# Two squared-sum passes of an eight-core sequence kernel wait for each 128-token block instead of the whole tile

## What is computed

```
x1  = x + W_out( h * silu-like gate of h )        # h from a recurrence over the tokens
y   = layernorm(x1)                               # mean and variance over 1024 features
hh  = rmsnorm(y, gamma1)                          # feeds Wq and Wdown/Wup
u   = y + ( attention over 16 heads ) @ Wo + bo
h2  = rmsnorm(u, gamma2)                          # mean of u*u over 1024 features
g   = softmax(h2 @ Wg)                            # 8 experts
out = x1 + u + sum_e g[e] * ( h2 @ We[e] )
```

## Time and profile before

| what | value |
|---|---|
| three timed runs | 3840.75, 3917.0, 3954.0 us (median 3917.0) |
| the profiled execution, own time | 3841.9 us |
| its span, slowest core (core 1) | 3840.0 us; the eight cores 3800.6 to 3840.0 us |
| TensorE matmul busy | 2512.3 us, 65% of the span |
| VectorE busy | 1468.3 us, 38% |
| ScalarE busy | 869.4 us, 23% |
| mean granted TensorE clock | 0.769 of full speed on core 1 |
| DMA | 319.70 MB, 83 GB/s on average |

### The profile page before, as it was taken

The page is one execution under the profiler, slowest core; times in us unless marked ns, Lnnn a source line. Parts: engine busy times, 40 slices in busy tenths (PEclk is TensorE's granted clock), DMA queues, the critical chain, the costliest instruction groups (busy, mean ns, idle before and its releaser), DMA issues.

```text
span 3840.0 us, 35132 instructions; the slowest of 8 cores (3800.6 to 3840.0 us)
## 1 busy us (share of the span) xinstructions
PE 2512.3 (65%) x12352; PEld 1180.1 (31%) x12352; DVE 1468.3 (38%) x1817; ACT 869.4 (23%) x1642; POOL 79.9 (2%) x143
## 2 busy tenths in 40 slices
PE   3556766557775587745976559664696647965578
PEld 1223322233332333223332234322243223432234
DVE  1343223453234433344333443245432363234532
ACT  2232003321123201232023320233103421024210
POOL 0000000000000000000000000000000000000000
PEclk9766888757887688866888669885698857987579
DMA  8631671301421013310233003320032201412012
GB/s 170 147 85 44 137 181 54 110 3 68 149 84 70 23 66 132 110 44 23 88 120 122 23 23 114 115 101 23 22 145 96 101 10 44 153 67 88 1 66 110
DMA packets 44455, 319.70 MB, mean 83 GB/s; under 512 B 5048, under 2 KB 5304, under 8 KB 28928
## 3 DMA queue, kind: packets, MB, share of 16 engines
q0 software_dynamic: 35040, 283.53, 23.7%
q1 hardware_dynamic: 9248, 33.91, 2.3%
HBM read 301.07 MB, written 48.23 MB: 91 GB/s over the span
## 4 chain that ended last, share of the span: by engine, by line
PE 52%; DVE 20%; DMA 11%; ACT 7%; issue 6%; DVEq 3%; ACTq 1%; POOL 0%; POOLq 0%; SPq 0%
PE bank L1432 21%; DMA w<-wscr 3%; PE bank L1146 3%; DMA w<-we 3%; PE bank L835 3%; PE bank L616 3%; PE bank L1372 3%; PE bank L442 3%; PE bank L488 3%; DVE vpu L929 3%; DVE kpot L929 2%; DVE sstat L1030 2%; PE bank L964 2%; PE bank L967 2%; DVE xph L1040 2%
## 5 line engine op out<-in xcount | busy, mean ns | idle before, releaser
L1432 PE MATMUL bank<-qpg,w 128*128 128x512 bf16 x4096 | 912.7, 387 | 86.6 <-DMA w<-we 44.4
L1432 PEld LDWEIGHTS bank<-qpg,w 128*128 128x128 bf16 x4096 | 405.8, 99 | 602.1 <-issue 137.2
L1405 DVE TENSOR_TENSOR qpg<-xph,ybuf 128x4096 bf16<-128x4096 bf16 x64 | 282.4, 4423 | 506.3 <-PE bank L1432 506.3
L1449 ACT ACTIVATE acomb<-bank 128x512 f32<-128x512 f32 x64 | 38.3, 598 | 1140.8 <-PE bank L1432 1136.7
L1016 ACT ACTIVATE hfm<-bank,sstat 128x128 bf16<-128x128 f32 x512 | 139.3, 383 | 529.4 <-DVE sstat L990 529.4
L1063 PE MATMUL bank<-cpb_s,xph 128*128 128x128 bf16 x512 | 64.8, 306 | 246.6 <-DVE xph L1040 246.6
L524 PE MATMUL bank<-xph,w 128*128 128x512 bf16 x512 | 133.2, 407 | 124.1 <-DMA w<-wscr 69.1
L616 PE MATMUL bank<-ln1g,w 128*128 128x512 bf16 x512 | 125.3, 410 | 96.1 <-DMA w<-wscr 75.7
L914 PE MATMUL bank<-zb,wupb 64*128 64x512 bf16 x128 | 73.2, 585 | 156.6 <-DVE vpu L929 112.0
L929 DVE TENSOR_SCALAR kpot<-bank,cph_s 64x512 bf16<-64x512 f32 x128 | 95.1, 743 | 196.4 <-PE bank L914 192.5
L990 DVE TENSOR_REDUCE sstat<-bank 128x4 f32<-128x512 f32 x128 | 82.5, 686 | 199.8 <-PE bank L967 199.8
(11 more groups left out here) (139 smaller groups left out, 2925.4 us busy)
## 6 DMA issues: line engine op xcount, KB each, us to landing
w<-wscr POOLq DMA_DIRECT2D x105, 2048.0 KB, 8.1
wscr<-w POOLq DMA_DIRECT2D x15, 2048.0 KB, 9.5
w<-we POOLq DMA_DIRECT2D x8, 2048.0 KB, 21.5
out<-ybuf SPq DMA_DIRECT2D x16, 1024.0 KB, 4.0
slotA<-x SPq DMA_DIRECT2D x4, 2048.0 KB
slotB<-x SPq DMA_DIRECT2D x4, 2048.0 KB, 13.5
w<-w_inT POOLq DMA_DIRECT2D x1, 2048.0 KB, 27.1
w<-w_aT POOLq DMA_DIRECT2D x1, 2048.0 KB, 22.7
```

The costliest lines, as they stand in the source:

```text
L1405: r = v.tensor_tensor(qpg[:, (e % 2) * 4096:(e % 2) * 4096 + 4096] .rearrange("p (c q) -> p c q", q=512), h2v[:, :, :], ybuf[:, e * 512:(e ...
L1432: last_pe = pe.matmul(bk[:, :], wslice(wbuf, kc, mc), qpg[:, (e % 2) * 4096 + kc * 512: (e % 2) * 4096 + (kc + 1) * 512], start=(e == 0 an ...
```

## The change

In `f_l2v` the one reduction over 128x4096 becomes four reductions over 128x1024, one per block, each behind a wait for that block's second add, `("x1", t, b, 1)`. They stand at the same place of VectorE's order as the one did, behind all eight adds. In `f_l2s` and in `f_us` the wait for the last add of the tile is replaced by a wait ahead of each square for the second add of its own block. Nothing else is touched: the squares, their outputs, the short statistics operations and all DMAs are as before.

```diff
             def f_l2v(v, t=t, xv=xv):
-                v.wait_ge(s_ve.h, tok[("x1d", t)])
-                r = v.tensor_reduce(
-                    sstat[:, S_S1:S_S1 + 4],
-                    xv[:, :].rearrange("p (b f) -> p b f", f=1024),
-                    axis=AX, op=OP.add)
+                for b in range(NBLK):
+                    v.wait_ge(s_ve.h, tok[("x1", t, b, 1)])
+                    r = v.tensor_reduce(
+                        sstat[:, S_S1 + b:S_S1 + b + 1],
+                        xv[:, b * 1024:(b + 1) * 1024],
+                        axis=AX, op=OP.add)
                 s_ve.inc(r)
                 tok[("ln2sum", t)] = s_ve.n
             block.vector(f_l2v)

             def f_l2s(s, t=t, xv=xv):
-                s.wait_ge(s_ve.h, tok[("x1d", t)])
                 for b in range(NBLK):
+                    s.wait_ge(s_ve.h, tok[("x1", t, b, 1)])
                     last_s = s.activation(out=trash_[b], in_=xv[:, b * 1024:(b + 1) * 1024],
...
             def f_us(s, t=t):
-                s.wait_ge(s_ve.h, tok[("ud", t)])
                 dwait(s, "d_ot")
                 for b in range(NBLK):
+                    s.wait_ge(s_ve.h, tok[("u", t, b, 1)])
                     s.activation(out=trash_[b],
```

## The result

The changed kernel runs at a median of 3817.65 us (16 runs), the kernel before at 3843.4 us (17 runs). The ratio is 0.9944, with a 95% interval of 0.9923 to 0.9965: 0.56% less, or some 21.5 us of 3843.4, between 13 and 30 us. The profiled execution took 3807.42 us with a span of 3805.5 us on its slowest core (core 2); the eight cores lie between 3784.0 and 3805.5 us.

The account below looks back on a forecast made before the run. The prediction saw no saturated engine but a chain of stages whose stalls are saved in full. -24.9 + 0.4 = -24.5 us, taken from the median 3917.0, gave 3892.5 us, with a range of 3806 to 3932.

Parts of the forecast that it names:

- Part 1: ScalarE's squares of u (`f_us`): block-wise waits start the last square earlier, saving 3.11 us a tile, 24.9 us in 8.
- Part 2: ScalarE's squares of x1 (`f_l2s`): end about 3.1 us earlier, worth nothing beside the reduction, up to 3 us without it.
- Part 3: VectorE's four reductions (`f_l2v`) after the x1 adds: 4.60 us together, taken as +0.05 us a tile, 0.4 us in all.
- The sum: Whole kernel: -24.9 us from the squares of u and +0.4 us from the four reductions make -24.5 us.
- the clock rival: Gate matmuls after u: a shorter stall keeps TensorE's clock up, 1.3 us a tile, 10.5 us more, 3882; chance 0.06.
- the upper end of the gain: Whole kernel: top of the forecast's own range from the bounds, a gain of 16 to 27 us.
- the first tile given back: First tile's experts: waits for expert weights absorb that tile's gain alone, 3895; losing most of the whole gain, chance 0.05.
- Small reductions: Rival at LN2 on VectorE: four unoverlapped 1.21 us reductions cost about +0.5 us a tile, gain 21 us, 3896; chance 0.10.
- the adds are not disturbed: Denies the rival that squares stretch VectorE's adds at x1 and u: at twice the length +41 us, 3958; chance 0.03.
- nothing was given back: Denies the rival that TensorE waits later for weight loads at a fixed date: all lost is 3917; losing most, chance 0.05.
- Within 2%: Whole kernel: measured time differs from before by under about 78 us, what a measurement can tell from no change; chance 0.95.
- The bound for the first tile: First tile's experts, which wait for expert weights: at most 3.1 us, one tile's gain, could be lost.

Follow-up runs that it names:

- `double_sq`: The changed kernel with a redundant second square, output unused, ahead of the squares of blocks 0, 1 and 2 of u; one run, 3821.85 us.
- `fused`: The changed kernel with each x1 add also giving its sum and one 128x4 add replacing the reductions; ratio 0.9847 to the kernel before.
- `fused_late_sq`: `fused` with the squares of x1 waiting for the whole tile again; one comparable run, 3822.98 us.
- run 17: Not a label but a count, in "run 17 times": the kernel before, without the change, timed 17 times; median 3843.4 us.
- `warm`: The changed kernel with 32 idle matmuls on constants on TensorE while ScalarE squares and scales u; ratio 0.9934 to the kernel before.

## Why the prediction was right and where it was wrong

**Part 1** was right in place and size: 3.11 us a tile predicted from the earlier trace rows, 3.12 us measured between the same two instructions. ScalarE kept pace with 0.41 us to spare, and `double_sq` shows what happens once it doesn't.

**Part 2** was right: the LN2 squares are worth nothing beside the reduction, and 3.12 us without it ("up to 3 us"), as `fused` and `fused_late_sq` show.

**Part 3** was right: 4.59 us from the first reduction's start to the last one's end against 4.60 predicted, and a net change at L714 of -0.01 us against +0.05. No working gives the +0.05: the sum ends at 708.42, at no change. The 1.21 us price taken from a bf16 reduction held for float32. The estimate from the Trainium skill (VectorE: DVE Perf Modes, The TRN2 errata), three more fixed terms at 0.47 us a tile, was too high for this sequence. The prediction's rows put the fixed part at 1.21 - 1.07 = 0.14 us, and it is there in each instruction's duration, but the next one starts inside it: each of the four starts 1.13 us behind the one before, 0.08 us before that one's end. So a further piece costs 0.06 us, and the four take 4.59 - 4.42 = 0.17 us more than the one, which the earlier start of the first makes good.

**The sum** of -24.5 us is well inside the measured 13 to 30 us and close to its middle of 21.5. The stretch that the edit touches gave -25.9 us. The gate matmuls account for the 0.9 us above part 1's 25.0: eight took 3.19 us on average before and 3.05 after (64 cases each). That is the clock rival in miniature, 0.14 us a tile instead of its 1.3. Two small slips change nothing: the upper end of the gain adds up to 24.9 + 1.4 = 26.3 us where the text has 27, and the first tile given back would be 3895.6, not 3895.

**The rivals** fell as their rows had suggested. Small reductions don't pay in full, the adds are not disturbed (684 ns with twice the squares), and nothing was given back. For the last one the prediction had read too little. It said that the later tiles show no wait for a weight load, which is true of the expert weights alone. TensorE also waits for the weights of W_out and of a gate matrix in each of the 7 later tiles, some 20 us a tile (kernel before; whole span):

```profile
PE bank L616 <- DMA w<-wscr: 75.7, 7, 11.1
...
PE bank L524 <- DMA w<-wscr: 69.1, 7, 11.2
```

These waits stayed (75.6 and 63.9 us in the changed kernel) and took nothing of the gain. Such a load is issued when TensorE frees a buffer, so it moves along with the chain.

**What failed is the step from the sum to the forecast, the choice of the base.** The prediction carried the change to the median of three runs, 3917.0, with the sentence "Nothing in the sum depends on which of these a run resembles, so I take it from the median", and so named 3892.5 us. The measured 3817.65 us is 75 us below it, three times the whole effect, and the forecast lies even above the kernel before as measured with more runs. The kernel before, run 17 times, has its median at 3843.4 us, near the lowest of those three runs. The profiled execution's own 3841.9 us was a better base than the median: from it the same sum gives 3817.4 us. That this is 0.3 us from the result is luck, for the comparable runs of the changed kernel lie between 3800.78 and 3839.17 us; that it is near is not. The evidence was in the text and was weighed wrongly: the profiled execution and one of three timed runs agreed to 1.2 us, while the other two differed from each other by 37.

The second error is of the same kind. The prediction took 2% as what a measurement can tell from no change. With 16 and 17 runs the interval is 0.42% wide, and 0.56% is clear of zero. "Within 2%" was right, but it says less than the runs can.

The third is small. The bound for the first tile was 3.1 us, its own share of the gain. Its expert stretch waits for weight loads that come from float32 matrices and take 21.5 us to land (2048 KB each in the buffer), where the later tiles' bf16 copies take 8.1. It ranged from 173.5 to 194.3 us over the cores of the kernel before, and its means lie between 176.8 and 189.2 us in the kernels of this study, in no order that the edits explain. A pair of profiles can differ by 7 us there alone, as the first pair did. What exactly sets the length of those loads is not settled here.

## What to carry to other kernels

A wait on "all blocks done" is worth shortening where the waiting engine ends last; find that engine first, for the same edit gave 3.12 us a tile in one place and nothing in the other, where a reduction of 4.4 us ran beside it. When a pass hides behind another, shortening the hidden one gains nothing and removing the longer one gains only their difference (0.15 us here); both together gave 3.27 us (19.93 to 16.66). An absolute forecast is better based on the profiled execution, if it agrees with the lowest runs, than on the median of three runs that lie 3% apart.

## What the runs showed of the hardware

A sum output on VectorE's adds was almost free: the 128x512 operation took 686 ns where the plain add took 685 (`fused`), and its accumulator read of 0.08 us ran beside the next one.

TensorE's clock can stay at its lower level while the engine is busy. In the changed kernel the eight-row float32 matmuls that broadcast the gates fill a stretch completely and are granted half of the clock from end to end (second tile, core 2):

```profile
878.80:892.70 13.90, 13.90 (x16) 4.76 (x16) 4.84 (x7) 0.00 (x0) 0.00 (x0) 0.50 0.00 0
```

That is 14 us a tile at 1.2 GHz, in all 64 cases of the kernels before and after and of `warm` alike (13.98 to 13.99 us, granted 0.50). What they would take at 2.4 GHz was not measured: the `warm` kernel kept the clock up for the transposes and in 18 cases for the gate matmuls, but never as far as these.

The same instructions at both levels, from `warm`: eight gate matmuls of 128x512 took 1.89 us at a granted 1.00, and eight of the transposes took 0.61 us where the changed kernel's took 1.01 at 0.50.
